# A linear-attention layer between two routers: the low part of the turned keys ahead of the decayed scores, and squares ahead of the weighted values in the last steps

## What is computed

```python
q = (hidden_states @ Wq.T).reshape(B, L, H, D)      # H 32 heads, KVH 8 key groups, D 128
k = (hidden_states @ Wk.T).reshape(B, L, KVH, D)
v = (hidden_states @ Wv.T).reshape(B, L, KVH, D)
...
scores = jnp.einsum('bhnid,bhnjd->bhnij', qc, kc)
decay = jnp.where(causal, jnp.exp(G[..., :, None] - G[..., None, :]), 0.0)
y_intra = jnp.einsum('bhnij,bhnjd->bhnid', scores * decay, xc)
k_dec = kc * jnp.exp(Glast - G)[..., None]
cstates = jnp.einsum('bhnjd,bhnje->bhnde', k_dec, xc)
def step(state, inp):
    dec, cs = inp
    return (state * dec + cs, state)
y_inter = jnp.einsum('bhnid,bhnde->bhnie', qc * jnp.exp(G)[..., None], prev)
y = (y_intra + y_inter).reshape(B, H, L, D).transpose(0, 2, 1, 3)
rms = jnp.sqrt(jnp.mean(jnp.square(y), axis=-1, keepdims=True) + RMS_EPS)
y = y / rms * gnorm_w
gate = (hidden_states @ Wg.T).reshape(B, L, H, D)
y = y * (gate * jax.nn.sigmoid(gate))
return y.reshape(B, L, H * D) @ Wo.T
```

## Time and profile before

| what | us |
|---|---|
| median of 3 runs | 1793.26 |
| lowest, highest | 1790.17, 1793.82 |
| the profiled execution's own time | 1792.12 |
| span of its instructions | 1790.3 |

### The profile page before, as it was taken

The page is one execution under the profiler, slowest core; times in us unless marked ns, Lnnn a source line. Parts: engine busy times, 40 slices in busy tenths (PEclk is TensorE's granted clock), DMA queues, the critical chain, the costliest instruction groups (busy, mean ns, idle before and its releaser), DMA issues.

```text
span 1790.3 us, 34879 instructions
## 1 busy us (share of the span) xinstructions
PE 1680.6 (94%) x11652; PEld 964.7 (54%) x11652; DVE 1442.7 (81%) x3157; ACT 1138.8 (64%) x3012; POOL 1209.0 (68%) x1139
## 2 busy tenths in 40 slices
PE   5667999999999999999999999999999999999976
PEld 4443555555555555555555555555555555555544
DVE  6984888888887878888897878787887888788876
ACT  5445666666666667666676666666766667666643
POOL 1225767776777768777777777776777768777633
PEclk9778999999999999999999999999999999999997
DMA  4110101110110101110121102110111111110002
GB/s 176 36 35 20 48 19 60 45 45 21 34 56 34 48 25 54 48 48 19 34 68 36 37 19 70 38 42 25 43 60 30 36 33 57 37 36 21 23 1 94
DMA packets 38481, 76.69 MB, mean 43 GB/s; under 512 B 4768, under 2 KB 5792, under 8 KB 37152
## 3 DMA queue, kind: packets, MB, share of 16 engines
q1 hardware_dynamic: 38304, 74.47, 13.2%
HBM read 69.99 MB, written 4.46 MB: 42 GB/s over the span
## 4 chain that ended last, share of the span: by engine, by line
PE 68%; POOL 15%; issue 7%; DVE 5%; ACT 5%; DMA 0%; SPq 0%; POOLq 0%; ACTq 0%; DVEq 0%
PE B L298 21%; PE B L300 21%; PE B L299 21%; PE B L784 3%; POOL WL L1099 3%; POOL QS L1105 2%; POOL PL L1140 2%; POOL ROWS L1118 1%; POOL WVF L1128 1%; POOL RR L1147 1%; POOL QL L1110 1%; ACT XN L417 1%; ACT QS L893 1%; ACT PF L931 1%; POOL WVL L1136 1%
## 5 line engine op out<-in xcount | busy, mean ns | idle before, releaser
L1140 POOL TENSOR_TENSOR PL<-PF,PH 128x512 bf16<-128x512 f32 x128 | 158.1, 1235 | 314.3 <-ACT PH L937 314.3
L298 PE MATMUL B<-WH,XTH 128*128 128x512 bf16 (+1 forms) x1024 | 282.6, 300 | 2.2 <-POOL WL L1099 2.2
L299 PE MATMUL B<-WL,XTH 128*128 128x512 bf16 (+1 forms) x1024 | 282.5, 300 | 0.0
L300 PE MATMUL B<-WH,XTL 128*128 128x512 bf16 (+1 forms) x1024 | 282.5, 300 | 0.0
L937 ACT ACTIVATE PH<-PF 128x512 bf16<-128x512 f32 x128 | 80.8, 631 | 276.0 <-DVE PF L1309 276.0
L298 PE MATMUL B<-XTH,WH 128*128 128x512 bf16 x640 | 243.3, 380 | 4.2 <-DVE QF L1275 3.5
L1105 POOL TENSOR_TENSOR QS<-QS,SIN 128x512 f32<-128x512 f32 x160 | 204.4, 1278 | 61.6 <-ACT QS L893 61.6
L299 PE MATMUL B<-XTL,WH 128*128 128x512 bf16 x640 | 243.3, 380 | 0.0
L300 PE MATMUL B<-XTH,WL 128*128 128x512 bf16 x640 | 243.1, 380 | 0.0
L1359 DVE SCALAR_TENSOR_TENSOR YF<-B,RR,G 128x128 f32<-128x128 f32 x512 | 144.0, 344 | 73.1 <-POOL RR L1147 73.1
L1309 DVE SCALAR_TENSOR_TENSOR PF<-B,DT,PF 128x128 f32<-128x128 f32 x512 | 143.4, 341 | 68.9 <-PE B L300 56.4
(11 more groups left out here) (158 smaller groups left out, 4464.8 us busy)
## 6 DMA issues: line engine op xcount, KB each, us to landing
ROWS<-rows_dram SPq DMA_DIRECT2D x128, 256.0 KB, 3.3
STAGE<-in_wall SPq DMA_DIRECT2D x112, 256.0 KB, 2.8
ACC<-in_x SPq DMA_DIRECT2D x4, 1024.0 KB, 9.4
out<-ACC SPq DMA_DIRECT2D x3, 1024.0 KB, 3.9
COS<-in_cos SPq DMA_DIRECT2D x1, 1024.0 KB, 13.7
SIN<-in_sin SPq DMA_DIRECT2D x1, 1024.0 KB, 16.4
out<-ACC SPq DMA_DIRECT2D x4, 256.0 KB, 2.0
EBF<-in_eb SPq DMA_DIRECT2D x1, 256.0 KB, 4.3
```

Of the source, the lines that this page charges most:

```text
L298: nc.tensor.matmul(out_, ah, bh, start=first, stop=False)
L299: nc.tensor.matmul(out_, ah, bl, start=False, stop=False)
L300: return nc.tensor.matmul(out_, al, bh, start=False, stop=last)
L1140: nc.gpsimd.tensor_tensor(PL[:, n % 2, :], PF[:, :], PH[:, n % 2, :], ALU.subtract).then_inc(pl_ready.sem, 1)
```

## The change

Two calls move. On DVE, in a block's last step (s = 3), `keys_lo(g, b + 1)` is called ahead of `decayed(g, n + 1)` instead of behind `add_out`. On ACT, in the last group's steps from n = 12 on (`ending`), `wv_hi(g, n + 1)` is called behind `square` and `state_hi` instead of ahead of them; it does something in n = 12 and 13 only, since the last chunk has no weighted values. No instruction is added or taken away, and no semaphore is changed.

```diff
@@ ScalarE's step
+                ending = last and n >= NCH - BLK
-                if nxt:
+                if nxt and not ending:
                     wv_hi(g, n + 1)
...
                 square(g, n)
                 state_hi(g, n)
+                if nxt and ending:
+                    wv_hi(g, n + 1)
@@ VectorE's step
+                if s == 3 and now:
+                    keys_lo(g, b + 1)
                 if nxt:
                     decayed(g, n + 1)
...
                 if s == 1 and now:
                     q_lo(g, b + 1, FILLS[0]["B"])
-                if s == 3 and now:
-                    keys_lo(g, b + 1)
                 scale_inter(g, n)
```

## The result

| | before | after |
|---|---|---|
| median of four runs each, us | 1793.47 | 1777.01 |
| lowest, highest | 1790.17, 1793.82 | 1776.81, 1779.69 |
| the profiled execution, us (its span) | 1792.12 (1790.3) | 1777.18 (1775.4) |

The changed kernel takes 0.9916 of the time of the kernel before, with a 95% interval of 0.9899 to 0.9933. Later, beside the experiments, the same code gave 0.9903 (0.9888 to 0.9918). The forecast was 1779.1, in a range of 1775.0 to 1784.0.

A forecast was written before the change was run, and what follows sets the result against it. The prediction took PE's matmuls plus a few places where PE stands to bound the loop. Its terms, 11.0 + 1.3 + 1.9 = 14.2 us, taken from 1793.26 gave 1779.1 us, range 1775.0 to 1784.0.

The forecast's parts named there:

- Step 3: In each of eight groups, PE's 1.38 us stall at turning the gated results, held by KDL, goes: 11.0 us.
- Step 11: In seven groups, the turning gains 0.18 us each, 1.3 us in all, though KDL delays PF by 0.60.
- Period: Sign in the step loop: a group's period is shorter by 1.38 + 0.18 = 1.56 us.
- The other 16 steps: Steps 7, 15 and the last group's 11: PE loses nothing to KDL now, idle DVE has room: 0 us.
- Part two: Last group's steps 12 and 13: earlier squares start the gated result 0.93 and 0.94 us earlier, 1.9 us in all.
- 1/rms (RM, then RR) ... can begin only 0.58 earlier: Last group's step 12 on POOL: the row mask limits 1/rms to 0.58 us earlier, RR ending at 1699.57 instead of 1700.15.
- waits for YF shorter by 0.93 and 0.94: Sign in the last steps: if the forecast is right, the waits for YF shrink by 0.93 and 0.94 us.
- The sum: Over the whole kernel: 11.0 + 1.3 + 1.9 = 14.2 us gained.
- (1): Rival, chance 0.08: POOL's WVF gives back gain in step 3, leaving 6.4 us, 1786.9 us.
- (2): Rival, chance 0.04: the turning has another release as late as KDL, so only 1.9 us gained, 1791.4 us.
- (3): Rival, chance 0.04: KDL ahead of PF holds the scores back, 31 x 0.60 us, net +4.4 us, 1797.7 us.

The follow-up runs named there:

- the two more instructions: Changed kernel with two more DVE instructions (statistics over the keys, results unused) right behind KDL in all 31 places: 1781.57 us, 0.9946 of the kernel before.
- the keys alone: Kernel before with only KDL (the keys' low part on DVE) moved, squares left in place: 1776.42 us, 0.9913 of the kernel before.
- the half dose: Kernel before with KDL put between PF and ACC, ahead of ACC but behind PF, squares unmoved: 1782.70 us, 0.9953 of the kernel before.
- earlier weights: Changed kernel with low parts of the next group's weights made earlier, on POOL in steps 2 and 13, on DVE in 13: 1776.45 us, 0.9921.
- the squares alone: Kernel before with only the squares moved ahead of the weighted values in the last group's steps 12 and 13: 1790.84 us, 0.9991.

## Why the prediction came right, point by point

- **Step 3.** The stall was sized at 1.38 and the gain is 1.43: a turning that had to wait held the next matmul back by 0.49, one that didn't by 0.44, which the trace of before showed and the working left out. KDL's place, the 0.30 us of idle time left, PF's unchanged start against ACT's decay and the 1.1 us at the next bank (1.04) are in the trace as forecast.
- **Step 11.** 0.18 was forecast and 0.23 came, by the same 0.05. The 0.60 by which PF is later there cost nothing, and the two more instructions show how near that was: the spare is less than 1.2 us. It lies not between PL and its use, where the prediction looked and counted 10 us, but on POOL, up to its weight of step 14.
- **Period.** 1.56 was forecast, 1.66 is measured; the loop gave 13.05 instead of 12.3.
- **The other 16 steps** give and take nothing, as forecast.
- **Part two is the term that failed in size**, 0.96 of 1.9. The step that failed is "1/rms (RM, then RR) ... can begin only 0.58 earlier", which took RR to follow RM by 0.28. With the squares earlier, RM meets STL on DVE, takes 0.65, and RR follows 0.73 later. That is 0.45 in each step, 0.90 of the 0.94 that are missing. The sign that was to show it, waits for YF shorter by 0.93 and 0.94, was badly chosen too: the waits for YF grew by 1.4, while those for STL fell by 2.3.
- **The sum** was 14.2 and is 14.0, and that it is so near is luck: an error of 0.75 in the loop and one of 0.94 in the last steps had opposite signs. The 2.5 more that lie between the medians (16.5) are within the 3 and 5 us by which the stretches ahead of and behind the loop vary.
- **Rivals.** (1) and (2) are out by the keys alone and by the half dose. (3) is out for this change, since from start to start no step of a group is longer than before; its mechanism exists, 0.46 per group once 1.2 us more stand ahead of PF, and reaches PE through POOL's weight in step 14, not through PL.
- **The rule of the Trainium skill on SBUF's ports** (SBUF — State Buffer, "Who interferes with whom") was tested in the prediction on KDL alone, and then dropped. KDL is 0.68 in its new place too. But the instruction that the change brought beside a new partner was STL, with two SBUF inputs, and there the rule decided.

## What to carry to other kernels

When a wait of the bounding engine is removed by reordering another engine in idle time that the timeline shows, the start-to-start stall on the bounding engine is the gain, to a few hundredths; look also for the turning point where that other engine stays busy for several steps on end, because a delay put in ahead of it comes out at its end. An engine that is on time by 0.06 us shows no idle time and is the next bound, so look at the releases of length zero too; here only the weight loads' view named it. Moving work earlier on DVE, which was full there, lost 0.22 in a group, and moving it to POOL, which had room, gained 0.81. And when an edit shifts two engines against each other, check which instructions with two SBUF operands come to stand beside GpSimd's.

## What the runs showed of the hardware

**A small GpSimd instruction waits for a VectorE instruction with two SBUF inputs.** In the changed kernel 49 of the 128 RM take 0.65 us, and all 49 start while DVE runs KF<-KF,QS (8), QF<-QF,QS (31) or STL<-ST,STH (10); in the row above RM ends at 1684.73, 0.06 after STL. The seven that start 0.06 ahead of an STL take 0.20, and so do the 14 that start directly behind another POOL instruction beside ZTL, whose operands are a PSUM tile, one SBUF tile and a column of scalars. It goes both ways with GpSimd instructions on 512 columns: that STL takes 1.01 instead of 0.69, as it started while the mask ran until 1684.12, and in the kernel with earlier weights QS takes 1.72 instead of 1.27 behind WL, and QL beside it 1.75. The Trainium skill, SBUF — State Buffer, section "Who interferes with whom", states that a VectorE instruction with two SBUF inputs and a GpSimd one that reads SBUF contend, and that the order of issue decides which of them blocks. The traces agree, with these numbers, but for one kind: of the changed kernel's STL, 64 start while an RR (128x4, 1.02 us) runs, and all of them keep 0.68 or 0.69. Where the STL is first, the RR behind it takes 1.33 or 1.34 (46 of 46).

**In some executions the granted clock falls for about 3 us in the last steps, and what that costs depends on the place.** Of the fourteen profiled executions nine show such a fall between step 12 of the last group and the projection behind the last turning, and five, the kernel before among them, show none. In the profiled execution of the changed kernel the clock fell 0.3 us after the start of the last turning, at which PE had stood 2.12 us:

```profile
1706.00:1709.00 3.00, 0.80 (x5) 0.66 (x6) 1.72 (x5) 0.34 (x1) 2.46 (x5) 0.92 0.00 0
1709.00:1712.00 3.00, 2.86 (x7) 1.06 (x7) 0.00 (x0) 3.00 (x5) 0.00 (x0) 0.51 0.02 5
```

The projection's matmuls follow each other every 0.43 us there, the lower level of 1.2 GHz, and every 0.22 behind it, at 2.4 GHz. From the start of that turning to the first turning of x it is 4.74 us, and 3.05 in the second trace of the same code, which has the same 2.12 and a clock of 1.00 there. In the kernels with the keys alone, the squares alone and the keys between, the fall came in step 13 (0.55 from 1688 to 1691 with the keys alone). With the keys alone it cost nothing: the last steps take 31.10 against 31.11 in the kernel before, which has no fall there, and the slower matmuls only fill PE's waits, which sum to 6.8 us (for YF and STL) instead of 8.5. Further falls come in the second router block. The two executions with the longest rest, 70.4 us each, are the two whose clock was low there for 23.9 us without a break. Why the falls come where they come is open.
